# The opening of a two-layer kernel: a new order on four engines, four sums moved to VectorE, scratch of its own for two rows

## The chip, the cores and the metric

One core of a Trainium2 chip. The metric is the device time of one execution in microseconds; before the change it is 1047.22 us, the median of 3 runs (1045.82 to 1048.94).

## The reference

The input is 4096 rows of 512 numbers (2 x 2048 x 512, float32). With LN a layer norm without weights:

```python
# attention layer
h = LN(x)
Q, V = h @ Wq.T + bq, h @ Wv.T + bv          # 16 heads of 32
logits = einsum('bhtd,lhd->bhtl', Q, latent) / sqrt(32)   # 64 latent keys
w = softmax(top_k(logits, 4))                 # weights of the 4 largest
a = einsum('bhtk,bhtkd->bhtd', w, selected latent rows) + V
x = x + LN(a @ Wo.T + bo)
# FFN layer, 512 -> 2048 -> 512
ternary(W) = clip(round(W / s), -1, 1) * s,   s = mean(|W|) + 1e-8
hid = silu(LN(x) @ ternary(W_up).T) * (LN(x) @ ternary(W_gate).T)
x = x + LN(hid @ ternary(W_down).T)
```

K is not used by the result.

## The kernel before

The rows are worked in 8 chunks of 512, a chunk being 4 tiles (t = 0 to 3) of 128 rows. One pass of the body does the attention of chunk i beside the FFN of chunk i - 1: "first" (attention of chunk 0 alone, called the opening here), "second", five passes "mid", "last" and "tail". The change touches "first" alone. To keep accuracy with float16 matmuls, each operand is split into a high and a low half (hi, lo): ScalarE (ACT) writes hi, GpSimd (POOL) or VectorE (DVE) writes lo as the difference, and TensorE (PE) adds three products.

Each engine has its order written out by hand in `body`, and semaphores link them: an engine runs its list strictly in order, so an instruction that waits holds all behind it. The parts of the opening, by the kernel's names:

- The first layer norm, the maxima of the weights and powers of two from them (`powers`, L1328), the splits of Wq, Wv, Wo (`weights_hi` L818 on ACT, `weights_lo` L1417 on DVE; index 0, 1, 2), Q in two halves of 256 rows (`q_half`), logits into PSUM (`logits`, L560), copied to Lb by ACT.
- The chain of a tile t on four engines. DVE: `maxes(t, b)` (8 MAX8 each, L1462), `slots(t)` (L1469, differences of the top four), `replace(t, b)` (8 MATCH_REPLACE8 each, L1484, marks the top four in Lr; after b = 1 it signals `replaced`), `sums(t)` (L1490 to L1500, needs `exp4(t)` of ACT), `select(t)` (L1505, needs `exps(t)`). POOL: `shift(t)` (L1170, after `replaced`), `normalise(t)` (L1177, after `select`), `probs_lo(t)` (L1160). ACT: `exp4(t)` (L904), `exps(t)` (L908, after `shift`), `probs_hi(t)` (L921, after `normalise`). SyncE (SP) then transposes the weights by DMA: `pt(t)`, L421. `probs_hi(2)` first waits for the transposes of tiles 0 and 1, and before the change `probs_hi(3)` for those of tiles 0 to 2.
- `v(m)` on PE (V of all rows), `weigh_half(h)` (L611, needs two transposed tiles each), `vw_half(m, h)` on ACT (L867, L871), `low_a_half(m, h)` on POOL (L1155), then `wo(t)` on PE (L646), the output projection: wo(0), wo(1) need the four `low_a_half(m, 0)`, wo(2), wo(3) the four of h = 1.
- On DVE `y_a(t)` (L1557 to L1565, reads wo(t)) and `y_b(t)` (L1577 to L1585, residual and statistics), between them `rstd_y(t)` on POOL, after them `rstd_x(0, t)` on POOL and `y_c(0, t)` on DVE, and the rows of the second norm (`t2_rows`, `t2_lo`, transposes L366).
- The rows of the next chunk: `ln1_stat(1)`, `ln1_rstd_of(1)` on POOL, `ln1_biases(1)`, then per tile `s1_rows(1, t)` on ACT (L777, L790), `s1_lo(1, t)` on POOL (L1206), and a transpose by SP (`s1`, L366) into XT. The second pass begins on PE with Q of chunk 1, which needs all four transposed tiles.
- The scales of the ternary weights: sums of magnitudes of 24 pieces of 128 x 1024 (`abs_sum(n)`; pieces 0 to 7 W_up, 8 to 15 W_gate). ACT does one as an activation with an accumulated sum (L838), DVE as a reduction (L1350). `tern_total(w)` adds eight pieces on DVE, `total` on PE adds over the partitions (L525), `tern_scale_of(w)` makes the scale, `round_to(n)` on DVE and `sign(n)` on ACT write a ternary piece. Q of the second pass also waits for `tern_scale_of(1)` (`tern_step` 2), for its bank of PSUM.

`split_buffers` gives the buffers of a row and its halves. Before the change tiles 2 and 3 of chunk 1 use those of tiles 0 and 1 again, so ACT waits for the low half of tile t - 2:

```python
elif kind == "first":
    wait(act, x_lo, i + c, TT, t - 1)
```

## Time and profile before

| what | value |
|---|---|
| median of 3 runs | 1047.22 us |
| the profiled execution, its time | 1049.91 us |
| its span in the profile | 1048.1 us |
| mean granted TensorE clock | 0.977 of full |

The profile is of one execution. Times in its rows are microseconds from the start of the span. An engine's idle time before an instruction stands in square brackets with what ended it; "issue" means that the profile shows nothing that it waited for. A busy PE may be at half clock; the granted clock tells.

### The profile page before, as it was taken

What the parts mean: (1) busy time and instruction counts of PE and PEld (TensorE: products, weight loads), DVE (VectorE), ACT (ScalarE), POOL (GpSimd) and SP (SyncE); (2) the same over time, 40 slices, a digit from 0 to 9 for tenths busy, and PEclk for the clock granted to TensorE, in tenths of its full rate; (3) what the DMA queues carried; (4) which work ended last, traced back from release to release, by engine and by line L of the source; (5) the groups of instructions that cost most, each with busy time, mean ns of one, the idle gap of its engine ahead of it and who ended that gap; (6) DMA issues with size and microseconds to landing.
All of it is one profiled execution on the core that took longest, in us unless ns stands there. A gap on an engine that the chain in (4) does not pass through costs nothing.

```text
span 1048.1 us, 17870 instructions
## 1 busy us (share of the span) xinstructions
PE 969.4 (92%) x5738; PEld 472.0 (45%) x5738; DVE 736.0 (70%) x2668; ACT 515.4 (49%) x803; POOL 542.8 (52%) x448
## 2 busy tenths in 40 slices
PE   2474998899999999999999999999999999989997
PEld 1331544345444454445444454445444454435443
DVE  6997889746993769836994768836894768835331
ACT  4867887245454355345444455345453445323321
POOL 2466346664565446554565446654566445633332
PEclk9786999999999999999999999999999999999999
DMA  8944502434115321243023321253023311212001
GB/s 252 395 101 91 162 1 61 113 89 101 19 23 102 71 71 20 50 110 91 13 38 89 76 76 20 40 119 92 11 40 72 88 31 21 41 41 62 1 0 41
DMA packets 149335, 76.94 MB, mean 73 GB/s; under 512 B 135825, under 2 KB 135825, under 8 KB 148113
## 3 DMA queue, kind: packets, MB, share of 16 engines
q1 hardware_dynamic: 149264, 76.18, 29.1%
q8 instruction: 23, 0.38, 0.1%
q14 instruction: 48, 0.39, 0.1%
HBM read 34.21 MB, written 8.39 MB: 41 GB/s over the span
## 4 chain that ended last, share of the span: by engine, by line
PE 76%; DVE 10%; issue 4%; ACT 4%; DMA 3%; POOL 2%; SPq 0%; POOLq 0%; DVEq 0%; ACTq 0%
PE ug L668 36%; PE ug L685 17%; PE ring L534 12%; PE ring L646 6%; PE ring L582 2%; DVE Lr L1484 2%; DMA PT<-halves 1%; PE ug L534 1%; PE ring L626 1%; DVE v L1462 1%; DVE ugt L1447 1%; ACT TU L844 1%; DMA x_in<-in_x 1%; DVE halves L1442 1%; ACT TG L844 0%
## 5 line engine op out<-in xcount | busy, mean ns | idle before, releaser
L1183 POOL TENSOR_TENSOR hT<-ugt,hT 128x512 f16<-128x512 f32 x128 | 168.0, 1312 | 164.2 <-ACT hT L953 164.2
L668 PE MATMUL ug<-X1T,TU 128*128 128x512 f16 (+1 forms) x1152 | 245.1, 356 | 7.2 <-DVE ugt L1452 6.3
L668 PE MATMUL ug<-X1T,TG 128*128 128x512 f16 (+1 forms) x1152 | 244.8, 355 | 0.0
L685 PE MATMUL ug<-TD,hT 128*128 128x512 f16 x960 | 213.6, 383 | 3.2 <-issue 3.2
L946 ACT ACTIVATE ugt<-ug,cu 128x512 f32<-128x512 f32 x128 | 87.9, 687 | 204.0 <-PE ug L668 203.2
L668 PEld LDWEIGHTS ug<-X1T,TU 128*128 128x128 f16 x1152 | 110.5, 98 | 116.1 <-DVE ugt L1452 5.5
L668 PEld LDWEIGHTS ug<-X1T,TG 128*128 128x128 f16 x1152 | 112.7, 98 | 108.6
L1447 DVE SCALAR_TENSOR_TENSOR ugt<-ugt,ug 128x512 f32<-128x512 f32 x128 | 87.3, 682 | 100.3 <-ACT ugt L946 99.4
L685 PEld LDWEIGHTS ug<-TD,hT 128*128 128x128 f16 x960 | 94.0, 99 | 120.6 <-issue 11.0
L1484 DVE MATCH_REPLACE8 Lr<-v,Lb 128x68 f32<-128x68 f32 x512 | 102.4, 213 | 0.2 <-issue 0.2
L1517 DVE BATCH_NORM_STATS2 stf<-ug 128x6 f32<-128x512 f32 x30 | 20.8, 694 | 109.3 <-PE ug L685 109.3
L1452 DVE SCALAR_TENSOR_TENSOR ugt<-ugt,ug 128x512 f32<-128x512 f32 x128 | 87.9, 687 | 4.4
L534 PE MATMUL ring<-XT,wq_hi 128*128 128x512 f16 (+1 forms) x288 | 80.5, 367 | 8.4 <-DVE wq_lo L1420 5.8
L1177 POOL TENSOR_TENSOR p<-Lb,r 128x1024 f32<-128x1024 f32 x32 | 60.8, 1901 | 48.3 <-issue 33.0
L1170 POOL TENSOR_TENSOR Lb<-Lb,v 128x1024 f32<-128x1024 f32 x32 | 62.3, 1947 | 44.4 <-DVE Lr L1484 44.4
L953 ACT ACTIVATE hT<-ugt 128x512 f16<-128x512 f32 x128 | 79.6, 622 | 3.7 <-DVE ugt L1452 3.7
L1462 DVE MAX8 v<-Lb 128x8 f32<-128x64 f32 x512 | 68.9, 210 | 0.4
L534 PE MATMUL ring<-XT,wv_hi 128*128 128x512 f16 x224 | 66.6, 379 | 0.0
L921 ACT ACTIVATE halves<-p 128x1024 f16<-128x1024 f32 x31 | 32.5, 1048 | 50.9 <-POOL p L1177 40.1
L534 PE MATMUL ring<-XT,wq_lo 128*128 128x512 f16 (+1 forms) x144 | 52.9, 367 | 0.0
L646 PE MATMUL ring<-wo_hi,qaT_hi 128*128 128x512 f16 x128 | 50.2, 392 | 2.5 <-POOL qaT_lo L1155 1.9
L804 ACT ACTIVATE xn<-x,nbx,rsx 128x512 f32<-128x512 f32 x28 | 22.7, 809 | 56.3 <-DVE nbx L1591 37.5
(193 smaller groups left out, 1464.8 us busy)
## 6 DMA issues: line engine op xcount, KB each, us to landing
out_dram<-Lr SPq DMA_DIRECT2D x32, 256.0 KB, 3.1
x_in<-in_x SPq DMA_DIRECT2D x7, 1024.0 KB, 5.5
x<-in_x SPq DMA_DIRECT2D x28, 256.0 KB, 3.3
PT<-in_Wd SPq DMA_DIRECT2D x8, 512.0 KB, 8.1
hT<-in_Wu SPq DMA_DIRECT2D x4, 512.0 KB, 9.4
hT<-in_Wg SPq DMA_DIRECT2D x4, 512.0 KB, 15.1
x_in<-in_Wd SPq DMA_DIRECT2D x4, 512.0 KB, 5.2
x_in<-in_x SPq DMA_DIRECT2D x4, 256.0 KB, 4.2
```

The costliest lines, as they stand in the source:

```text
L534: last = pe.matmul(bank[:, cols], wT[w][a][:, k, m * P:(m + 1) * P], XT[:, b, k, cols], start=(n == 1), stop=(stop and n == 3 * KD), skip_ ...
L646: last = pe.matmul(ring[:, bank, :], qaT[a][:, k, t * P:(t + 1) * P], wT[2][b][:, k, :], start=(n == 1), stop=(n == 3 * KD))
L668: last = pe.matmul(ug[:, 2 * (e % 2) + s, cols], w[:, k, e * P:(e + 1) * P], X1T[:, b, k, cols], start=(k == 0 and b == 0), stop=(k == KD ...
L685: last = pe.matmul(down_bank(kind, t), hT[:, a, e, t * P:(t + 1) * P], td[:, e, :], start=(e == 0 and a == 0), stop=(e == NE - 1 and a == 1))
L946: act.activation(ugt[:, e % 2, :], ug[:, 2 * (e % 2), :], ACT.Tanh, scale=cu[:, 0:1]).then_inc(tanh_ready, 1)
L953: act.activation(hT[:, 0, e, :], ugt[:, 2 + e % 2, :], ACT.Copy).then_inc(h_hi, 1)
L1170: pool.tensor_tensor(buf, buf, v8[:, t % 2, :, 0:1].broadcast_to([P, H, NL]), ALU.subtract).then_inc(shifted, 1)
L1183: pool.tensor_tensor(hT[:, 1, e, :], ugt[:, 2 + e % 2, :], hT[:, 0, e, :], ALU.subtract).then_inc(h_lo, 1)
L1447: dve.scalar_tensor_tensor(out=ugt[:, e % 2, :], in0=ugt[:, e % 2, :], scalar=1.0, in1=ug[:, 2 * (e % 2), :], op0=ALU.add, op1=ALU.mult).t ...
L1452: dve.scalar_tensor_tensor(out=ugt[:, 2 + e % 2, :], in0=ugt[:, e % 2, :], scalar=HS, in1=ug[:, 2 * (e % 2) + 1, :], op0=ALU.mult, op1=ALU ...
L1462: last = dve.max(v8[:, t % 2, h, :], Lb[:, t % 2, h, 0:NL])
L1484: last = dve.match_replace(Lr[:, h, :], v8[:, t % 2, h, :], Lb[:, t % 2, h, :], HIT)
```

## The change

- **DVE:** `sums(t)` stands between `replace(t, 0)` and `replace(t, 1)`; `weights_lo(1)` moves ahead of `select(0)`, `latV_lo` to behind `replace(1, 1)`, `weights_lo(2)` to behind `replace(3, 1)`. The sums of pieces 12 to 15 come from ACT to DVE, behind `select(3)` and `ln1_biases(1)`; `y_a(0)` and `y_a(1)` stand ahead of `tern_total(0)`, `y_a(2)` and `y_a(3)` ahead of `tern_total(1)`.
- **ACT:** `exp4(0)` ahead of `logits(1)`, the remaining sums spread anew, the rows of tiles 2 and 3 ahead of `vw_half(m, 1)`, with no wait for buffers, and a wait for two transposes ahead of `sign(0)`.
- **POOL:** `shift(3)` behind `probs_lo(2)` and ahead of all `low_a_half(m, 0)`; `normalise(3)` between the first and the last two of these; `rstd_x(0, 0)` between `low_a_half(1, 1)` and `low_a_half(2, 1)`, `rstd_x(0, 1)` between `s1_lo(1, 2)` and `s1_lo(1, 3)`.
- **PE:** the second `total` of the guards ahead of `logits(0, 1)`; `weigh_half(1)` ahead of the total of W_up; the total of W_gate behind `wo(3)`.
- **Buffers:** tiles 2 and 3 of chunk 1, and the weights of attention of tile 3, lie in parts of TU, which is free until `sign(0)`.

```diff
--- before.py
+++ after.py
@@ -262,8 +262,8 @@
         junk = xn[:, :].bitcast(F16)
         late_junk = ring[:, 0:2, :].rearrange("p b t -> p (b t)")
 
-        ASUM_DVE = (0, 1)
-        ASUM_ACT = (16, 17, 18, 19) + tuple(range(2, 16)) + tuple(range(20, 24))
+        ASUM_DVE = (0, 1, 12, 13, 14, 15)
+        ASUM_ACT = (16, 17, 18, 19) + tuple(range(2, 12)) + tuple(range(20, 24))
         TERN_ORDER = (0, 8, 1, 9, 4, 12, 2, 10, 5, 13, 3, 11, 6, 14, 22, 23, 16, 17, 7, 15, 20, 21, 18, 19)
 
         def after_tern(*pieces):
@@ -298,6 +298,8 @@
             if kind == "first" and c == 0:
                 return (qaT[t // 2][:, :, :].rearrange("p k t -> p (k t)").bitcast(F32)[:, (t % 2) * D:(t % 2 + 1) * D],
                         PT[:, 0, 2 * t:2 * t + 2, :].rearrange("p k t -> p (k t)"))
+            if kind == "first" and t >= 2:
+                return TU[:, 2 * D * t:2 * D * t + 2 * D].bitcast(F32), TU[:, 2 * D * t + 4 * D:2 * D * t + 6 * D]
             if kind == "first":
                 return Lb[:, t % 2, 0:D // NL, 0:NL], out_buf[t % 2].bitcast(F16)
             return xn[:, :], halves[:, t % 2, :]
@@ -306,6 +308,8 @@
 
             if kind == "first" and t == 1:
                 return row[:, :, :].rearrange("p a d -> p (a d)").bitcast(F16).rearrange("p (s d) -> p s d", s=2)
+            if kind == "first" and t == 3:
+                return TU[:, 0:4 * D].rearrange("p (s d) -> p s d", s=2)
             return halves[:, :, :]
 
         def wide(v, rows):
@@ -692,9 +696,9 @@
                     for m in range(KD):
                         q_half(m, 0)
                     q_half(0, 1)
-                    logits(0, 1)
                     pe.wait_ge(qa32_ready, KD)
                     total(guard_sums(1), mg[:, 2:4], mg_ready, 2, ma_ready)
+                    logits(0, 1)
                     q_half(1, 1)
                     q_half(2, 1)
                     pe.wait_ge(sc_step, 7)
@@ -705,14 +709,14 @@
                     weigh_half(0)
                     wo(0)
                     wo(1)
+                    weigh_half(1)
                     wait(pe, l_ready, i, 8, 8)
                     total(weight_sum(0), tot[:, 0:1], tot_ready, 1, tota_ready)
-                    weigh_half(1)
-                    wait(pe, y_ready, i, TT, 1)
-                    total(weight_sum(1), tot[:, 1:2], tot_ready, 2, tota_ready)
                     wo(2)
                     pe.wait_ge(tern_step, 1)
                     wo(3)
+                    wait(pe, y_ready, i, TT, 1)
+                    total(weight_sum(1), tot[:, 1:2], tot_ready, 2, tota_ready)
                     return
                 if att:
                     for m in range(KD):
@@ -768,7 +772,7 @@
 
                         wait(act, p_ready, i, TT, 3 + t)
                     elif kind == "first":
-                        wait(act, x_lo, i + c, TT, t - 1)
+                        pass
                     elif t:
                         wait(act, x_lo, i + c, TT, t)
                     else:
@@ -783,6 +787,8 @@
                     elif kind == "first" and t < 2:
 
                         wait(act, p_raw, i, TT, TT)
+                    elif kind == "first":
+                        pass
                     elif t < 2:
                         wait(act, p_t, i + c, 16 * TT, 0)
                     else:
@@ -796,7 +802,7 @@
                     if t:
                         wait(act, x1_lo, i + c, TT, t)
                     elif kind == "first":
-                        act.wait_ge(asum_done, ASUM_ACT.index(2 * NPIECE - 1) + 1)
+                        act.wait_ge(asum_done, ASUM_ACT.index(11) + 1)
                     elif nxt:
                         wait(act, x_lo, i + 1, TT, TT)
                     else:
@@ -913,7 +919,7 @@
                     if kind == "first" and t == 1:
                         act.wait_ge(latV_split[1], 1)
                         wait(act, scales, 0, 1, 2)
-                    elif t:
+                    elif t and not (kind == "first" and t == 3):
                         wait(act, p_t, i, 16 * TT, 16 * t)
                     for s in range(2):
                         if t == 0 and ffn:
@@ -972,54 +978,51 @@
                     q_half(1, 1)
                     q_half(2, 1)
                     q_half(3, 1)
+                    exp4(0)
                     logits(1)
-                    exp4(0)
                     weights_hi(1)
                     exps(0)
                     latV_hi()
                     abs_sum(16)
+                    exp4(1)
                     abs_sum(17)
-                    exp4(1)
                     probs_hi(0)
                     logits(2)
                     abs_sum(18)
-                    weights_hi(2)
                     exps(1)
                     abs_sum(19)
-                    abs_sum(2)
-                    abs_sum(3)
                     exp4(2)
-                    abs_sum(4)
-                    abs_sum(5)
+                    weights_hi(2)
                     probs_hi(1)
                     logits(3)
-                    abs_sum(6)
-                    abs_sum(7)
+                    abs_sum(2)
                     exps(2)
-                    abs_sum(8)
+                    abs_sum(3)
+                    abs_sum(4)
                     exp4(3)
+                    abs_sum(5)
+                    probs_hi(2)
                     vw_half(0, 0)
                     vw_half(1, 0)
+                    exps(3)
                     vw_half(2, 0)
                     vw_half(3, 0)
-                    probs_hi(2)
-                    exps(3)
-                    abs_sum(9)
-                    abs_sum(10)
-                    abs_sum(11)
-                    abs_sum(12)
                     probs_hi(3)
                     s1_rows(1, 0)
                     s1_rows(1, 1)
-                    abs_sum(13)
-                    abs_sum(14)
-                    abs_sum(15)
+                    abs_sum(6)
+                    abs_sum(7)
+                    s1_rows(1, 2)
+                    s1_rows(1, 3)
                     vw_half(0, 1)
                     vw_half(1, 1)
                     vw_half(2, 1)
                     vw_half(3, 1)
-                    s1_rows(1, 2)
-                    s1_rows(1, 3)
+                    abs_sum(8)
+                    abs_sum(9)
+                    abs_sum(10)
+                    abs_sum(11)
+                    act.wait_ge(x_t[0], 32)
                     sign(0)
                     t2_rows(0, 0)
                     sign(8)
@@ -1223,25 +1226,29 @@
                     shift(1)
                     probs_lo(0)
                     normalise(1)
+                    shift(2)
                     probs_lo(1)
-                    shift(2)
                     normalise(2)
-                    for m in range(KD):
-                        low_a_half(m, 0)
+                    probs_lo(2)
                     shift(3)
-                    probs_lo(2)
+                    low_a_half(0, 0)
+                    low_a_half(1, 0)
                     ln1_rstd_of(1)
                     normalise(3)
+                    low_a_half(2, 0)
+                    low_a_half(3, 0)
+                    probs_lo(3)
                     rstd_y(0)
-                    probs_lo(3)
-                    rstd_y(1)
                     s1_lo(1, 0)
                     s1_lo(1, 1)
+                    rstd_y(1)
+                    low_a_half(0, 1)
+                    low_a_half(1, 1)
                     rstd_x(0, 0)
+                    low_a_half(2, 1)
+                    low_a_half(3, 1)
+                    s1_lo(1, 2)
                     rstd_x(0, 1)
-                    for m in range(KD):
-                        low_a_half(m, 1)
-                    s1_lo(1, 2)
                     s1_lo(1, 3)
                     rstd_y(2)
                     rstd_y(3)
@@ -1352,8 +1359,8 @@
             def tern_total(w):
                 pieces = range(NPIECE * w, NPIECE * w + NPIECE)
                 dve.wait_ge(asum_done, max(ASUM_ACT.index(n) + 1 for n in pieces if n in ASUM_ACT))
-                if w == 0:
-                    dve.wait_ge(own_asum, len(ASUM_DVE))
+                if w < 2:
+                    dve.wait_ge(own_asum, (2, len(ASUM_DVE))[w])
                 dve.reduce_sum(tot[:, w:w + 1], asum[:, NPIECE * w:NPIECE * w + NPIECE], AX.X).then_inc(tot_ready, 1)
 
             def tern_scale_of(w):
@@ -1616,50 +1623,52 @@
                     maxes(0, 1)
                     slots(0)
                     replace(0, 0)
+                    sums(0)
                     replace(0, 1)
                     maxes(1, 0)
                     maxes(1, 1)
-                    sums(0)
+                    weights_lo(1)
                     select(0)
                     slots(1)
                     replace(1, 0)
+                    sums(1)
                     replace(1, 1)
-                    weights_lo(1)
+                    latV_lo()
                     maxes(2, 0)
                     maxes(2, 1)
-                    sums(1)
                     select(1)
                     slots(2)
                     replace(2, 0)
+                    sums(2)
                     replace(2, 1)
-                    latV_lo()
-                    weights_lo(2)
                     maxes(3, 0)
                     maxes(3, 1)
-                    sums(2)
                     select(2)
                     slots(3)
                     replace(3, 0)
+                    sums(3)
                     replace(3, 1)
+                    weights_lo(2)
                     ln1_stat(1)
+                    select(3)
+                    ln1_biases(1)
+                    for n in range(12, 16):
+                        abs_sum(n)
+                    y_a(0)
+                    y_a(1)
                     tern_total(0)
-                    sums(3)
-                    select(3)
-                    y_a(0)
-                    ln1_biases(1)
-                    y_a(1)
                     tern_scale_of(0)
                     round_to(0)
                     y_b(0)
                     y_b(1)
-                    tern_total(1)
                     y_c(0, 0)
                     y_c(0, 1)
+                    y_a(2)
+                    y_a(3)
+                    tern_total(1)
                     tern_scale_of(1)
                     round_to(8)
-                    y_a(2)
                     t2_lo(0, 0)
-                    y_a(3)
                     y_b(2)
                     t2_lo(0, 1)
                     y_c(0, 2)
```

## Rows read from the trace of the kernel before

**Rows 1.** The head of the page and its busy times.

```profile
span 1048.1 us, 17870 instructions
...
PE 969.4 (92%) x5738; PEld 472.0 (45%) x5738; DVE 736.0 (70%) x2668; ACT 515.4 (49%) x803; POOL 542.8 (52%) x448
```

**Rows 2.** Stretches: PE, PEld, DVE, ACT, POOL busy (x), PEclk, DMA share, GB/s.

```profile
78.00:104.00 26.00, 11.33 (x85) 5.22 (x84) 18.59 (x43) 20.98 (x35) 16.61 (x17) 0.71 0.49 92
...
104.00:130.00 26.00, 26.00 (x190) 15.24 (x188) 21.20 (x42) 22.12 (x31) 9.90 (x8) 0.96 0.53 163
```

**Rows 3.** Chain that ended last, opening: start us, us, what.

```profile
71.06 7.45 PE ring L646 x24
...
89.94 0.91 PE ug L611 x18
...
96.10 1.17 POOL Lr L1206
...
98.83 3.11 DMA XT<-Lr
...
102.19 12.22 PE ring L534 x48
```

**Rows 4.** Timeline of DVE, opening: start us, us, instruction, idle before it.

```profile
27.86 1.21 DVE L1350 TENSOR_REDUCE asum<-ugt 128x1 f32<-128x1024 f32 x1
...
31.61 2.12 DVE L1462 MAX8 v<-Lb 128x8 f32<-128x64 f32 x16
...
34.06 0.09 DVE L1484 MATCH_VALUE_LOAD Lr<-v,Lb 128x8 f32 x1
...
37.24 2.12 DVE L1462 MAX8 v<-Lb 128x8 f32<-128x64 f32 x16
...
53.34 0.20 DVE L1490 TENSOR_REDUCE s<-d 128x16 f32<-128x64 f32 x1
...
53.96 1.16 DVE L1505 SCALAR_TENSOR_TENSOR Lb<-Lr,Lb 128x1024 f32<-128x1024 f32 x1
```

**Rows 5.** Line L1420, the low halves of the weights: duration ns min/median/max.

```profile
L1420 DVE SCALAR_TENSOR_TENSOR wv_lo<-TG,upw,wv_hi x4: 740/1580/2609, 45.1 to 50.7; 128x512 f16<-128x512 f32 x4
...
L1420 DVE SCALAR_TENSOR_TENSOR wo_lo<-TG,upw,wo_hi x4: 747/747/747, 59.1 to 61.1; 128x512 f16<-128x512 f32 x4
```

**Rows 6.** Timeline of POOL beside those instructions.

```profile
45.28 2.37 POOL L1170 TENSOR_TENSOR Lb<-Lb,v 128x1024 f32<-128x1024 f32 x1 [1.55 <-DVE Lr L1484]
...
47.61 2.57 POOL L1160 TENSOR_TENSOR halves<-p,halves 128x1024 f16<-128x1024 f32 x1
...
60.44 3.42 POOL L1160 TENSOR_TENSOR row<-p,row 128x1024 f16<-128x1024 f32 x1 [3.28 <-ACT row L921]
```

**Rows 7.** Timeline of ACT: the copies of logits(1).

```profile
35.28 1.25 ACT L898 ACTIVATE Lb<-ug,clo 128x512 f32<-128x512 f32 x2
```

**Rows 8.** Line L421, transposes of the weights of attention.

```profile
DMA to landing us min/median/max: 4.3/4.4/9.4
```

**Rows 9.** Timeline of POOL, end of the opening.

```profile
70.25 1.48 POOL L1155 TENSOR_TENSOR qaT_lo<-x_kept,qaT_hi 128x256 f16<-128x256 f32 x2
...
73.44 1.93 POOL L1170 TENSOR_TENSOR Lb<-Lb,v 128x1024 f32<-128x1024 f32 x1
...
83.14 2.12 POOL L1160 TENSOR_TENSOR halves<-p,halves 128x1024 f16<-128x1024 f32 x1 [1.74 <-ACT halves L921]
...
88.56 0.98 POOL L1124 TENSOR_TENSOR rsx<-vax,nh 128x1 f32<-128x1 f32 x1
```

**Rows 10.** Timeline of DVE, rows of the output projection and of the second norm.

```profile
78.78 0.74 DVE L1557 SCALAR_TENSOR_TENSOR row<-ring,clo,bo_b 128x512 f32<-128x512 f32 x1
...
80.84 0.74 DVE L1557 SCALAR_TENSOR_TENSOR row<-ring,clo,bo_b 128x512 f32<-128x512 f32 x1
...
85.74 0.74 DVE L1577 SCALAR_TENSOR_TENSOR x<-row,rsy,x 128x512 f32<-128x512 f32 x1
...
87.66 1.49 DVE L1577 SCALAR_TENSOR_TENSOR x<-row,rsy,x 128x512 f32<-128x512 f32 x1
```

## The prediction

> **What bounds the kernel.** I read the page first: PE is busy for 92% of the span [rows 1]. That says little of the opening, so I cut the start into stretches: from 78 to 104 us PE works 11.33 of 26 us, at a granted clock of 0.71 (part of it at 1.2 GHz, not 2.4), while from 104 to 130 us it is busy all through, at 0.96 [rows 2]. The border is the start of Q of chunk 1 at 102.19. What the change can win is therefore how much earlier that start comes; everything behind it moves with it, as long as PE has its inputs. The chain says what ends last before it: the transposed weights of tiles 2 and 3 let PE do `weigh_half(1)` at 89.94, and behind it come ACT, POOL's `s1_lo` at 96.10, and the transpose issued at 98.83 that lands 3.11 later [rows 3]. The weights of tile 3 hang on `probs_lo(3)`, which POOL starts at 83.14, and that on `shift(3)` at 73.44 [rows 9], at the end of four tiles' work in line on DVE.
>
> Third, the timelines of DVE and POOL, for waits that are no idle time. The four low halves of Wv take up to 2609 ns each, those of Wo 747 [rows 5]. Beside Wv's lie two POOL instructions of 2.37 and 2.57 us [rows 6], where the same kinds take 1.93 and 2.12 alone [rows 9]. Operations of DVE with two operands in SBUF and operations of POOL take turns: one stands while the other runs. Maxima, replacements and reductions show no such stretch.
>
> **Part by part.** I walk the chain anew, each time a start or an end in the changed kernel.
>
> *Start.* PE makes the guard's total before the logits, so `powers(1)` is done before the first copy of logits lands; `maxes(0)` starts at about 31.0, not 31.61. Maxima and slots take 2.45, sixteen replacements 3.18, so half of them 1.6; sums 0.6; select 1.2 [rows 4]. Half of tile 0 is replaced at 35.0. `sums(0)` now stands there and waits for `exp4(0)`, which ACT can start where `logits(1)` stood, at 35.28 [rows 7]: done at 35.5. With sums 36.2, second half 37.8, against 37.24 before [rows 4]. The move costs 0.5 here.
>
> *`weights_lo(1)`.* `maxes(1)` ends at 39.9. The splits follow while POOL waits for `select(0)`, so they take 2.7, as Wo's did [rows 5], not the 6.3 from 45.1 to the end of the last: done at 42.6. V can start 9 us earlier. I price that at nothing: V is used by `weigh_half(0)`, which waits for `pt(1)`. The price is paid by `select(0)`: 43.8, then tile 1 is replaced at 43.8 + 0.3 + 1.6 + 0.6 + 1.6 = 47.9, against 45.28 for the shift that it releases [rows 6].
>
> *Tiles 1 to 3.* `shift(1)` from 48.0, held 0.25 by `latV_lo`, ends at 50.2; `exps(1)`, some 1.1, at 51.3. POOL is then in `probs_lo(0)` until 52.3, and `select(1)` has two SBUF operands: it ends at 53.2, before at 55.1 [rows 4]. Tile 2 is replaced at 53.2 + 4.1 = 57.3, `shift(2)` ends at 59.4, `probs_lo(1)` at 61.5; `select(2)` is held by it and ends at 62.5; tile 3 is replaced at 66.6. `logits(3)` stands behind the splits of Wo on ACT, but `select(2)` comes later than its maxima either way, so I cost that at nothing.
>
> *The meeting at 67.* `pt(1)` is issued at 61.65 and lands after 4.4 [rows 8], at 66.1; `probs_hi(2)` ends at 67.1. POOL now has `probs_lo(2)` ahead of `shift(3)`, and DVE is in `weights_lo(2)` from 66.6 to 69.3. Two outcomes are in the trace. (B) DVE keeps the port through its four: `probs_lo` beside Wo's splits took 3.42 instead of 2.12, so it stood 1.3 us, longer than one split of 0.75 [rows 5, 6, 9]. Then `probs_lo(2)` ends at 71.3 and `shift(3)` at 73.3, 2.1 earlier than before. (A) They alternate, as at 45 us: `shift(3)` ends at 71.9, but the splits at 73.5, and `ln1_stat(1)` and `select(3)` behind them end at 77.7. I take B: it is the same pair of instructions. The Trainium skill (SBUF — State Buffer, Who interferes with whom) says that whoever issues first holds the pair for the whole instruction and the other blocks; taken strictly, the turn would pass after each split, which is A, and Q would come at 102.3 to 103.3. The trace bears it out at 45 us and not at 60.
>
> *Out of the chain, by B.* `exps(3)` 74.4; two `low_a_half` 1.5 [rows 9], 74.8; `select(3)` 76.0; POOL's `ln1_rstd_of(1)`, 1.0 as its like [rows 9], 77.0; `normalise(3)`, as long as a shift, 78.9; the other two `low_a_half` 80.4; `probs_lo(3)` 82.5, before 85.3 [rows 9]. `probs_hi(3)` no longer waits for a transpose: the wait was in the old 83.14. `pt(3)` lands at 87.0, `weigh_half(1)` ends at 87.9, before 90.85 [rows 3]: 2.9 won.
>
> *Four sums on DVE.* 4 x 1.2 [rows 4] from 77.1 to 81.9. Behind them wait `y_a(0)`, `y_a(1)` and the total of W_up. PE ends `wo(0)` at about 82 (`low_a_half(3, 0)` at 80.4 is its last input) and `wo(1)` at 86: 24 matmuls took 7.45, the first of them at half clock [rows 3], and these start from idle too. So the sums cost nothing; `y_a(1)`, 2.0 [rows 10], ends at 88.0, and the total at 88.2 meets the end of `weigh_half(1)`. On ACT four sums less are hidden: it waits for `weigh_half(1)`.
>
> *Where the gain goes.* Rows 2 and 3 of chunk 1 no longer wait on ACT, but `s1_lo(1, 2)` stands on POOL behind `low_a_half(3, 1)`, and that behind `rstd_x(0, 0)`, which needs `y_b(0)`, `round_to(0)` and the total of W_up. 88.4 total, 88.9 scale, 90.0 rounded (with 0.4 of port), `y_b(0)` 1.9 [rows 10] and 0.4, 92.3; `rstd_x` 1.0, 93.3; two `low_a_half` 94.8; `s1_lo` 1.17 [rows 3], 96.0; `rstd_x` 0.8, 96.8; `s1_lo` 98.0. The last transpose is issued at 98.2 instead of 98.83: Q could start at 101.5. The other condition of Q is new in place: `tern_scale_of(1)` comes after `wo(3)` and `y_a(3)`. `wo(2)` ends at 96.0; `wo(3)` at 97.9 at full clock or 99.9 at half; then 2.0 for `y_a(3)` and 0.8 for total and scale: 100.8 to 102.7. I take Q at 102.0, 0.2 earlier. By A each step from `select(3)` on is 0.7 to 1.4 later: Q at 102.3 to 103.3.
>
> **Sum.** The profiled execution took 1049.91 us around its span of 1048.1 [rows 1]; 0.2 less is 1049.7. The median of the three runs is 2.7 lower, so against it the forecast is 1047.22 - 0.2 = 1047.0. A measurement of this kernel can tell about 0.3% from no change, 3.1 us.
>
> **Rivals.** (1) *Faster: the collisions don't happen.* If `select(1)`, `select(2)` and `probs_lo(2)` each get the port at once, `pt(3)` lands up to 4 us earlier than I have it, `wo` and the rest behind it too, and Q starts at 98. That is 4.2 less; and PE would idle less before Q, so up to 1 us of its half clock goes [rows 2]. 1043.0 to 1042. For it: DVE's own work in line shrinks by the 3.6 us of Wv. Against it: new placements put DVE's two-operand work beside POOL's three times.
>
> (2) *Slower: the total of W_gate becomes the bound.* Place: PE's list, `total` behind `wo(3)`, DVE's `y_a(3)` ahead of `tern_total(1)`. It decides from the point where `wo(3)` ends later than 99.4, and each us beyond is a us of time. If A comes, `y_b(0)` is held by the port as well and `wo(2)`, `wo(3)` run at half clock (the 24 in 7.45 had half clock for some 4 us; the other 3.4 would double [rows 3]), `wo(3)` ends at 102.5 and Q starts at 105.4: 3.2 more, 1050.4. For it: `wo(2)` now gets its inputs in two pairs with `rstd_x` between, so PE idles inside it. Against: B, and a clock that was up in half of this stretch [rows 2].
>
> (3) *A instead of B:* 0.1 to 1.1 more, 1047.3 to 1048.3, within what counts as the same. This is also the sentence on the skill's rule.
>
> (4) The change does what it says, but the second pass, with roundings and tiles on DVE, gives or takes another 1 us by the same port; that is in the range.
>
> **Numbers.** B 0.40, A 0.22, rival 1 0.22, rival 2 0.16. Same is B and A, 0.62; faster 0.22; slower 0.16. The range takes the forecast with 1.5 us of unknown on each side of A and B, and reaches to rival 1's upper half and to rival 2's price with 0.6 above it: 1042.5 to 1051.0.
>
> **What would show it.** Splits of Wv of 0.75 each from 40 us and V at 43. `select(1)` longer than 1.2. POOL's `probs_lo(2)` at 67 of over 4 us (B), or `weights_lo(2)` spread over 7 us (A). `probs_lo(3)` ending at 82.5, `weigh_half(1)` at 87. `rstd_x(0, 0)` with POOL idle before it, released by DVE. Q at 101.5 to 102.7, released by the scale or the transpose about alike. I am wrong if Q starts before 99 or after 105, or if it starts where I say and the time differs by over 3 us all the same: then the second pass made it.

## The result and the profile after

The changed kernel took 1050.76 us (median of 8 runs, 1049.45 to 1052.49), the kernel before beside it 1047.93 (8 runs, 1045.82 to 1049.64): a ratio of 1.0028, 95% interval 1.0019 to 1.0038. Run again as `after_again` (11 runs, beside other runs of before) it took 1050.84 and the ratio was 1.0018 (1.0009 to 1.0027). One run of before in that batch, of 2652.3 us, was slow and is left out of the ratios. The change makes the kernel slower by 2 to 3 us. I had forecast 1047.0, no difference. Line numbers from L1120 on are now 3 to 7 higher.

The head of the page after, with its busy times:

```profile
span 1048.6 us, 17859 instructions
...
PE 969.0 (92%) x5738; PEld 470.9 (45%) x5738; DVE 739.3 (71%) x2672; ACT 510.7 (49%) x795; POOL 542.5 (52%) x448
```

It answers to [rows 1] and tells nothing: no engine's work has changed by more than 5 us. The profiled execution took 1050.42 us, only 0.5 more than that of before, against 2.8 in the medians. So I did not compare whole spans. Two things blur them. The kernel's first work starts at another time in each execution (the first norm's `rs` in POOL between 8.40 and 9.89 us over all my profiles), and far behind the change some executions have a short stretch at a lower granted clock. Stretch 920 to 925 us, in before, after and after_again (PE, PEld, DVE, ACT, POOL busy, PEclk, DMA share, GB/s):

```profile
920.00:925.00 5.00, 4.02 (x54) 1.50 (x55) 0.00 (x0) 2.97 (x5) 1.61 (x2) 0.69 0.19 63
```
```profile
920.00:925.00 5.00, 1.99 (x51) 0.90 (x51) 0.00 (x0) 0.91 (x2) 0.00 (x0) 1.00 0.69 155
```
```profile
920.00:925.00 5.00, 2.32 (x48) 0.94 (x48) 0.00 (x0) 0.75 (x2) 0.00 (x0) 0.76 0.59 136
```

In all three PE has just waited some 3 us for transposed weights; PE's row behind that wait, before and then after:

```profile
920.98 0.63 PE L626 MATMUL ring<-PT,latV_hi 64*32 64x512 f16 x16 [3.00 <-DMA PT<-halves]
```
```profile
923.15 0.63 PE L630 MATMUL ring<-PT,latV_hi 64*32 64x512 f16 x16 [3.02 <-DMA PT<-halves]
```

Behind this wait the granted clock fell in before and after_again and not in after, and the change touches nothing there. Before's profile lost about 1.6 us by it: counted as below, its lead over after is 2.66 us at the output store near 802 us and 1.04 at the last. From here on I count each mark of a profile from the start of that first `rs` (before 9.89, after 9.39, after_again 9.69):

```
us from the start of the first rs      before   after   after_again
weigh_half(1) on PE                     80.05   78.59    78.72
first matmul of Q of chunk 1            92.30   94.52    94.75
first sign of the second pass (ACT)    105.80  108.15   108.40
first store of the output              197.75  200.05   200.30
```

The opening gains 1.5 us up to `weigh_half(1)` and then loses 3.7 before Q. From Q on the 2.2 us stay, 2.3 at the first store, and that is the size of the ratio. Where they arise stands in the chain that ended last, 66 to 104 us, after (start us, us, what):

```profile
66.53 6.60 DVE wo_lo L1427 x4
73.12 2.39 DVE st L1404 x4
...
76.24 1.14 DVE Lb L1512
...
77.41 0.83 POOL rs L1127
78.24 1.86 POOL p L1180
80.11 0.64 POOL qaT_lo L1158
...
80.79 6.12 PE ring L650 x18
...
93.49 1.00 POOL rsx L1127
94.49 0.64 POOL qaT_lo L1158
...
95.17 5.76 PE ring L650 x18
...
102.90 0.17 DVE tot L1364
```

In [rows 3] the chain went over `weigh_half(1)`, `s1_lo` and a transpose to Q. Now it enters DVE at the four splits of Wo, 6.60 us where they took 2.73 before, goes on through what stands behind them, then over PE's `wo(2)` and `wo(3)`, and ends at the total of W_gate. Three rows of PE's timeline show the price at the end of it (start us, us, instruction, idle before it and who ended that):

```profile
95.17 0.61 PE L650 MATMUL ring<-wo_hi,qaT_hi 128*128 128x512 f16 x1 [2.11 <-POOL qaT_lo L1158]
103.21 0.35 PE L529 MATMUL ring<-tot,ones 128*128 128x1 f32 x2 [2.29 <-DVE tot L1364]
103.91 0.59 PE L538 MATMUL ring<-XT,wq_hi 128*128 128x512 f16 x2 [0.34 <-DVE sw L1369]
```

PE stands 2.11 us inside `wo(2)`, then 2.29 for `y_a(3)` and the sum behind it, and 0.34 for the scale: Q follows the scale, not the transposes (the last is issued near 98.6 and lands some 3.0 later, at about 101.6). The stretches of [rows 2], after:

```profile
78.00:104.00 26.00, 15.70 (x95) 6.10 (x96) 19.57 (x42) 18.89 (x32) 16.45 (x19) 0.73 0.40 62
104.00:130.00 26.00, 24.92 (x188) 14.75 (x188) 22.12 (x36) 22.64 (x32) 9.75 (x8) 1.00 0.63 172
```

PE does 4.4 us more in the first stretch than before, and yet Q starts later: `wo(0)` and `wo(1)`, which ran at 71 to 78 us before, now wait for `normalise(3)` and what follows it on POOL (4.70 us, until 80.79) and lie in it too.

The splits and POOL beside them. Line L1427, duration ns min/median/max, then POOL's timeline, then DVE's, all after:

```profile
L1427 DVE SCALAR_TENSOR_TENSOR wv_lo<-TG,upw,wv_hi x4: 731/742/743, 39.5 to 41.5; 128x512 f16<-128x512 f32 x4
...
L1427 DVE SCALAR_TENSOR_TENSOR wo_lo<-TG,upw,wo_hi x4: 746/1783/2609, 66.4 to 72.0; 128x512 f16<-128x512 f32 x4
```
```profile
66.99 2.17 POOL L1163 TENSOR_TENSOR halves<-p,halves 128x1024 f16<-128x1024 f32 x1 [2.56 <-ACT halves L927]
69.12 2.38 POOL L1173 TENSOR_TENSOR Lb<-Lb,v 128x1024 f32<-128x1024 f32 x1
71.46 2.19 POOL L1158 TENSOR_TENSOR qaT_lo<-x_kept,qaT_hi 128x256 f16<-128x256 f32 x2
```
```profile
66.44 0.75 DVE L1427 SCALAR_TENSOR_TENSOR wo_lo<-TG,upw,wo_hi 128x512 f16<-128x512 f32 x1
...
71.97 1.15 DVE L1427 SCALAR_TENSOR_TENSOR wo_lo<-TG,upw,wo_hi 128x512 f16<-128x512 f32 x1
...
76.15 1.22 DVE L1512 SCALAR_TENSOR_TENSOR Lb<-Lr,Lb 128x1024 f32<-128x1024 f32 x1
78.28 1.85 DVE L1416 SCALAR_TENSOR_TENSOR nb<-mv,rs 128x4 f32<-128x4 f32 x1 [0.91 <-POOL rs L1127]
80.05 4.58 DVE L1357 TENSOR_REDUCE asum<-hT 128x1 f32<-128x1024 f32 x4
```

Read the four splits against POOL: the first runs alone (0.75); the second stands through `probs_lo(2)`, the third through `shift(3)`, the fourth for part of a `low_a_half` (1.15). The four of Wv, moved to 39.5 us, take 2.72 instead of 6.28: that part of the change does what it should. The row at 78.28 is a surprise: four elements a partition, 1.85 us, all through POOL's `normalise(3)` (78.21 to 80.11).

### The profile page after: what moved, and what is told of

Same layout as the page of the kernel before. It is cut to its first block, busy times and chain, and to the rows that moved or that the text cites. A ratio compares the mean times of both kernels' runs of the same rounds, so it can differ in the third digit from the quotient of the medians.

```text
span 1048.6 us, 17859 instructions
## 1 busy us (share of the span) xinstructions
PE 969.0 (92%) x5738; PEld 470.9 (45%) x5738; DVE 739.3 (71%) x2672; ACT 510.7 (49%) x795; POOL 542.5 (52%) x448
## 4 chain that ended last, share of the span: by engine, by line
PE 64%; DVE 17%; issue 6%; ACT 5%; POOL 5%; DMA 3%; POOLq 0%; SPq 0%; DVEq 0%; ACTq 0%
PE ug L672 33%; PE ug L689 13%; PE ring L538 9%; PE ring L650 6%; DVE Lr L1491 3%; PE ring L586 2%; DVE ugt L1454 1%; DMA PT<-halves 1%; DVE Lb L1512 1%; DVE v L1469 1%; POOL halves L1209 1%; DVE stx L1587 1%; DVE halves L1449 1%; DVE x L1584 1%; DVE row L1564 1%
## 5 line engine op out<-in xcount | busy, mean ns | idle before, releaser
L689 PE MATMUL ug<-TD,hT 128*128 128x512 f16 x960 | 211.3, 380 | 3.2 <-issue 3.2
L1491 DVE MATCH_REPLACE8 Lr<-v,Lb 128x68 f32<-128x68 f32 x512 | 102.3, 211 | 0.0
L1173 POOL TENSOR_TENSOR Lb<-Lb,v 128x1024 f32<-128x1024 f32 x32 | 62.5, 1953 | 48.1 <-DVE Lr L1491 48.1
L538 PE MATMUL ring<-XT,wv_hi 128*128 128x512 f16 x224 | 66.6, 379 | 0.0
L650 PE MATMUL ring<-wo_lo,qaT_hi 128*128 128x512 f16 x128 | 50.8, 397 | 0.0
```

What stands on the lines that cost most here:

```text
L538: last = pe.matmul(bank[:, cols], wT[w][a][:, k, m * P:(m + 1) * P], XT[:, b, k, cols], start=(n == 1), stop=(stop and n == 3 * KD), skip_ ...
L650: last = pe.matmul(ring[:, bank, :], qaT[a][:, k, t * P:(t + 1) * P], wT[2][b][:, k, :], start=(n == 1), stop=(n == 3 * KD))
L689: last = pe.matmul(down_bank(kind, t), hT[:, a, e, t * P:(t + 1) * P], td[:, e, :], start=(e == 0 and a == 0), stop=(e == NE - 1 and a == 1))
L1173: pool.tensor_tensor(buf, buf, v8[:, t % 2, :, 0:1].broadcast_to([P, H, NL]), ALU.subtract).then_inc(shifted, 1)
L1491: last = dve.match_replace(Lr[:, h, :], v8[:, t % 2, h, :], Lb[:, t % 2, h, :], HIT)
```

## The experiments

**after_again** is the changed kernel itself, beside e1 to e3; its numbers stand above.

> The changed kernel as it is, on this chip, as the yardstick of the other three. Q of chunk 1 starts at 103.9 us in its first profile, 1.7 later than before, and what follows keeps that: 1.5 to 3 us slower than before in the median.

All ratios are against before, run beside each kernel. "From rs" means the marks of the table above. The theory: (a) the turn-taking at 67 us makes `select(3)` late, and (b) `wo(3)`, `y_a(3)` and the total of W_gate, now behind one another, carry that to Q. The rivals: the four sums on DVE, the second pass, POOL's order.

**e1_splits_in_gap**, against (a): Wo's splits go between `sums(3)` and the last eight replacements, when POOL has little to do.

```diff
 sums(3)
+weights_lo(2)
 replace(3, 1)
-weights_lo(2)
```

> weights_lo(2) ahead of replace(3, 1), where POOL waits for the transpose. Theory 1 (the meeting of weights_lo(2) with probs_lo(2) and shift(3) cost DVE 4 us in the chain): the four splits take 2.7 us instead of 6.7, select(3) ends about 3.5 us earlier, weigh_half(1) comes at about 84 instead of 88, and Q at about 100. Rival (the total of W_gate behind wo(3) sets the start of Q by itself, through ACT's last magnitude sums, which end at 97.4): Q gains under 1 us. Time by theory 1: 3 to 4 us less than the changed kernel.

Ratio 0.9986 (0.9977 to 0.9995), median 1047.14. The splits take 2.65 us, `weigh_half(1)` is at 75.07 from rs and Q at 91.34, 3.2 earlier than in the changed kernel. So the alternation costs 3.2 us of Q, and 0.3 to 0.4% of the time (0.9986 against 1.0018 and 1.0028). One list entry turns the change from a loss to a small gain. The marks of the one profile show the loss gone but no gain over before: Q is 1.0 us earlier, the first sign (105.93) and the first store (197.87) stand where before's do. Part (b) is still there, PE waits 2.28 for the total:

```profile
99.85 0.56 PE L529 MATMUL ring<-tot,ones 128*128 128x1 f32 x2 [2.28 <-DVE tot L1364]
100.75 1.01 PE L538 MATMUL ring<-XT,wq_hi 128*128 128x512 f16 x2 [0.34 <-DVE sw L1369]
```

**e2_total_early**, against (b): on PE the total goes ahead of `wo(3)`, on DVE the sum, scale and rounding ahead of `y_a(3)`.

```diff
 wo(2)
-pe.wait_ge(tern_step, 1)
-wo(3)
 wait(pe, y_ready, i, TT, 1)
 total(weight_sum(1), ...)
+pe.wait_ge(tern_step, 1)
+wo(3)
...
+tern_total(1)
 y_a(2)
-y_a(3)
-tern_total(1)
 tern_scale_of(1)
 round_to(8)
+y_a(3)
```

> The total of W_gate ahead of wo(3) on PE, tern_total(1) ahead of y_a(2) on DVE, the scale and round_to(8) between y_a(2) and y_a(3). Theory 2 (Q waits for the scale alone, the transposed rows have landed before): Q starts at 101.9 to 102.2, when the last transpose of chunk 1's rows lands, 1.8 us earlier, and the time is 1.8 us less than the changed kernel, about that of before. Rival (the time of the second norm's rows or of the second pass decides, not Q): no change.

Q is at 92.35 from rs and the first sign at 106.07, both 2.1 to 2.2 earlier than in the changed kernel. The timed ratio does not show it: 1.0017 (1.0006 to 1.0028), median 1049.72 with runs from 1047.73 to 1052.87. So the profile says that (b) holds Q by 2.2 us; that it is worth 2.2 us of time is not shown by this run. In the profile the gain stays: the store near 802 us is 2.44 earlier from rs than in after, the last store 1.67 earlier than in after_again, which like e2 has the lower clock at 920. Before Q, PE now waits 0.97 for DVE's reading of `wo(3)` in `y_a(3)`.

**e3_both**, e1 and e2 together.

> Both edits. If both theories hold, the transposed rows come at about 98 and the scale is not later: Q at 98 to 99.5, 4 to 5.5 us less than the changed kernel and 2 to 3.5 less than before. If the magnitude sums of ACT, which now wait less, still end at about 95 and hold the total, Q comes at 99 or later.

Ratio 0.9982 (0.9973 to 0.9991), median 1046.59; Q at 90.34 from rs, first sign at 105.20, first store at 197.12. The gains do not add. The total of W_gate now waits 0.91 for ACT's own sums. In the second pass PE's first FFN matmuls wait 1.13 for the transposed rows of the second norm (0.91 in the changed kernel), and the later ones, at 120.71, 1.16 for a product that DVE makes from their results (0.17 there): a second queue is right behind the first.

**d1_no_dve_sums**, the rival of the sums. The kernel leaves the four sums of `abs_sum(12)` to `(15)` out, and the scale of W_gate is made from ACT's four alone.

```diff
-for n in range(12, 16):
-    abs_sum(n)
```

> The changed kernel without the four magnitude sums on DVE; the scale of W_gate is then made from the other four sums alone. Theory (they lie beside PE's wo(0) and wo(1) and cost nothing): y_a(1) starts when wo(1) ends, as now, Q at about 103.9, no change of time. Rival (they are in the chain): up to 4.6 us less before y_a(0), Q up to 2 us earlier.

Ratio 1.0019 (1.0010 to 1.0027); Q at 94.51 from rs, against 94.52 with the sums. `y_a(0)` and `y_a(1)` only wait for PE instead (3.44 and 1.57 us in place of 0 and 0.40). The 4.58 us of sums cost nothing, as forecast, and this rival falls.

**d2_before_wv_ahead**, one part of the change alone: before, with Wv's splits ahead of `select(0)`.

```diff
 sums(0)
+weights_lo(1)
 select(0)
...
 replace(1, 1)
-weights_lo(1)
```

> The kernel before with one part of the change alone: weights_lo(1) ahead of select(0). Theory (port): the four splits of Wv take 2.7 us instead of 6.3, so maxes(2) starts at about 47.5 instead of 51.3; select(1) may meet probs_lo(0) and lose 1; tile 3 is done 2.5 to 3.5 us earlier, weigh_half(1) at about 87, Q at 99 to 100, 1.5 to 3 us less than before. Rival (the transposes and ACT hold tile 3 anyway): no change.

Ratio 0.9986 (0.9977 to 0.9995), median 1047.35; Q at 91.53 from rs, 0.8 earlier than before. This one move alone is as good as e1, the whole change with its fault mended. It fell short of its expectation all the same: Wv's splits take 2.65 in place of 6.28, but `weigh_half(1)` is only 0.8 earlier from rs (79.26), where Q was to come 2 to 3 us earlier. Where the rest went isn't shown. It also gives a second case like [rows 6], in POOL's and DVE's rows:

```profile
58.63 2.96 POOL L1160 TENSOR_TENSOR row<-p,row 128x1024 f16<-128x1024 f32 x1 [3.74 <-ACT row L921]
```
```profile
L1420 DVE SCALAR_TENSOR_TENSOR wo_lo<-TG,upw,wo_hi x4: 743/743/745, 56.9 to 58.9; 128x512 f16<-128x512 f32 x4
```

POOL asks in the third split (58.20 on) and stands some 0.8 us, through the fourth: none of the four is held. So [rows 5, 6] were no accident of one profile, and yet the same pair came out the other way at 67 us.

**d3_low_a_ahead**, POOL's order: the changed kernel, with the inputs of `wo(2)` ahead of the second norm's root.

```diff
-rstd_x(0, 0)
 low_a_half(2, 1)
 low_a_half(3, 1)
+rstd_x(0, 0)
```

> The changed kernel with low_a_half(2, 1) and (3, 1) ahead of rstd_x(0, 0) on POOL. Theory (wo(2) and with it the total of W_gate hang on POOL's place behind the statistics of y_b(0)): wo(2) runs without its gap of 2.1 us, wo(3) ends 2 to 2.5 us earlier at about 98.5, Q at 101.5 to 102, 1.5 to 2.4 us less than the changed kernel. Rival: ACT's last magnitude sums (97.4) and the rows' transposes hold Q, under 1 us.

Ratio 0.9997 (0.9987 to 1.0007), median 1047.93; Q at 93.13 from rs, 1.4 earlier. The hole of 2.11 us inside `wo(2)` is gone (0.26), and 1.3 us of it come back as a longer wait for the total:

```profile
100.99 0.56 PE L529 MATMUL ring<-tot,ones 128*128 128x1 f32 x2 [3.59 <-DVE tot L1364]
101.89 1.01 PE L538 MATMUL ring<-XT,wq_hi 128*128 128x512 f16 x2 [0.34 <-DVE sw L1369]
```

So three steps share the loss, and each of e1, e2 and d3 takes one away: 3.2, 2.2 and 1.4 us of Q, more in sum than the 2.2 lost against before, as they lie in one line and overlap.

**f1_reordered**, what follows for the kernel. From e3: both totals on PE between `weigh_half(1)` and `wo(2)`; ACT's sums spread over its earlier waits, its `t2_rows(0, 0)` ahead of the first sign; on POOL `s1_lo(1, 2)` and both `low_a_half` ahead of `rstd_x(0, 0)`, and the roots of tiles 2 and 3 in the order of their tiles; on DVE, as a diff against e3:

```diff
 tern_total(0)
+tern_total(1)
+y_b(0)
 tern_scale_of(0)
+tern_scale_of(1)
 round_to(0)
-y_b(0)
+round_to(8)
 y_b(1)
...
```

> A version of its own, from e3_both: ACT does four more magnitude sums where it waits for POOL, so that both totals are made together behind y_a(1); low_a_half(2, 1), (3, 1) and the rows of chunk 1 ahead of rstd_x(0, 0) on POOL; t2_rows(0, 0) ahead of sign(0); t2_lo(0, 0) and y_b(2) ahead of y_a(3) on DVE. Theory: what follows e3 is held by the order, not by work: wo(3) ends at 95, Q at 95 to 97, 2 to 4 us less than e3_both, 3.5 to 5.5 less than before. Rival: the second norm's rows and DVE's roundings in the second pass take most of it back, under 1 us less than e3_both.

Ratio 0.9960 (0.9947 to 0.9973), median 1043.96; Q at 87.93 from rs, 4.4 earlier than before, the first store 3.7 earlier. Faster than both kernels.

**f2_last_tile_first**, f1 with `s1_lo(1, 3)` ahead of `rstd_x(0, 0)` as well.

> The reordered kernel (f1), with s1_lo(1, 3) also ahead of rstd_x(0, 0) on GpSimd, because its Q began at 97.32 us after a wait of 2.04 us for the transposes of those rows. Theory (the rows of the last tile set Q there): s1_lo(1, 3) ends 1.0 us earlier, Q starts near 96.3, and the first sign of the second pass is up to 1 us earlier: 0.995 to 0.996 against before. Rival (second norm's rows set what follows Q): Q starts earlier, but the first sign of the second pass does not, as rstd_x(0, 0) is 1.15 us later, and the time is that of f1 or up to 1 us longer.

Ratio 0.9951 (0.9937 to 0.9965), median 1043.22. Q at 86.78 from rs, first sign at 101.48, 1.15 and 0.65 earlier than in f1: the theory. The two ratios overlap, so that f2 beats f1 is shown by the marks alone. PE's row of Q, and the stretches, f2:

```profile
96.05 0.59 PE L538 MATMUL ring<-XT,wq_hi 128*128 128x512 f16 x2 [1.54 <-DMA XT<-TU]
```
```profile
78.00:104.00 26.00, 21.35 (x129) 8.91 (x128) 22.41 (x54) 17.36 (x30) 14.95 (x17) 0.88 0.50 82
```

PE is busy 21.35 us of the stretch where the changed kernel had 15.70, at a granted clock of 0.88 in place of 0.73. The transposes end last before Q again, as in [rows 3].

**x3_shift_ahead**, the last rival: is it POOL's order, `shift(3)` behind `probs_lo(2)`, rather than DVE's?

```diff
-probs_lo(2)
 shift(3)
+probs_lo(2)
```

> The changed kernel, with shift(3) ahead of probs_lo(2) on GpSimd. Theory (the lost time is that of VectorE's four splits and of ln1_stat behind them): the splits still take about 6.6 us beside GpSimd's two large operations, ln1_stat still ends near 76 and select(3) stays at 76, so the ratio stays that of the changed kernel, 1.001 to 1.004 against before. Rival (the lost time is that of GpSimd's order, shift(3) behind probs_lo(2)): select(3) starts 2 us or more earlier, near 73.5, and the ratio falls to 1.000 or less.

The splits take 6.68 us again, `select(3)` starts at 76.32; ratio 1.0012 (1.0002 to 1.0021), within the changed kernel's. So what makes `select(3)` late is DVE's own queue, splits and `ln1_stat(1)`. (This profile has its first sign 2.5 us later than the changed kernel's, from rs, where Q is 1.5 later; the timed runs show no such loss.)

**x1_request_in_first_split** and **x2_request_in_third_split** ask what decides who gets the turn, by one profile each. x1 is an edit of before, x2 of the changed kernel, whose last eight replacements are cut into heads 8 to 10 and 11 to 15:

```diff
 latV_lo()
-weights_lo(2)
 maxes(3, 0)
+weights_lo(2)
```
```diff
 sums(3)
-replace(3, 1)
+replace(3, 1, 8, 11)
 weights_lo(2)
+replace(3, 1, 11, 16)
```

> The kernel before, with maxes(3, 0) moved in front of weights_lo(2), so that GpSimd's probs_lo(1), which asked for its turn at 60.44 us between the second and the third of the four splits of Wo and then waited through them, now asks in the first split (splits at about 60.2 to 62.8 if they are not held). Theory P (the place of the request in the run of splits decides): as in the changed kernel at 66.99 us, probs_lo(1) starts at once and ends near 62.6, and the four splits take 6 to 7 us in place of 2.73. Rival B (this kernel's DVE keeps its turn whatever the place, the changed kernel differs by something else): the splits take 2.7 us and probs_lo(1) lasts more than 4 us.

> The changed kernel, with the second replacing of tile 3 cut in two (heads 8 to 10, the four splits of Wo, heads 11 to 15), so that the splits start about 1 us earlier and GpSimd's probs_lo(2) asks at about 67.0 us in the third of them. Theory P (place decides): the splits take 2.7 us, probs_lo(2) waits about 1 us for the fourth to end, shift(3) starts near 70 and select(3) near 75.6. Rival (the changed kernel's other moves decide): probs_lo(2) starts at once, the splits that are left alternate with GpSimd, wo_lo takes 5 us or more and select(3) starts after 78.

x1 missed its aim: the maxima waited 1.89 us for ACT, so `probs_lo(1)` started beside an idle DVE at 60.31, and it was `shift(2)` that asked in the first split. It was let in behind it, and one split stood 2.42: 4.65 us in all, and Q 1.4 us later than before (93.66 from rs). Its one time is 1050.91, beside a median of 1048.59 for before. x2 hit it, and theory P falls:

```profile
66.71 2.52 POOL L1163 TENSOR_TENSOR halves<-p,halves 128x1024 f16<-128x1024 f32 x1 [2.55 <-ACT halves L927]
```
```profile
L1427 DVE SCALAR_TENSOR_TENSOR wo_lo<-TG,upw,wo_hi x4: 742/744/2608, 65.2 to 67.2; 128x512 f16<-128x512 f32 x4
```

POOL asked in the third split (66.51 on), stood 0.4 us, and the fourth stood 1.9 for it. In d2 it asked in the third as well and waited through the fourth. So the place in the run doesn't decide. Nor does the time left in it: POOL asked 0.11 us before DVE's next split in after and 0.46 in x2, and was let in, 0.23 in d2, and was not. What x2 does show is the price per turn: with `shift(3)` kept out of the splits (its tile was not marked yet) they take 4.59 instead of 6.68, and Q comes at 92.67 from rs, 1.9 earlier than in the changed kernel: 2.1 us off the splits, 1.9 off Q. Its one time is 1047.44.

## Why the prediction was wrong

**Right, up to 67 us.** The walk met the trace within about 0.4 us: Wv's splits 2.72 (2.7), `shift(1)` 47.57 to 49.7 (48.0 to 50.2), `select(1)` to 52.9 (53.2), `shift(2)` from 57.30 (57.3), `probs_lo(1)` to 61.3 (61.5), `select(2)` to 62.4 (62.5), the splits of Wo from 66.44 (66.6). Both `select` were held, 2.06 and 2.04 us, so rival 1 had no basis. `sums(0)` waited for ACT and cost what I gave it. V ended earlier, but `weigh_half(0)` stood 10.49 us of idle time behind it, so this gave nothing.

**The step that failed: "The meeting at 67", "I take B: it is the same pair of instructions."** The trace of before had this pair come out one way at 45 us and the other at 60, and I let the nearer likeness decide, 0.40 to 0.22. What the runs showed was A, in all five profiles that keep this order (the two of the changed kernel, e2, d1, d3: 6.68 or 6.69 us for the four splits), and in x3 with the order turned. The Trainium skill's rule (SBUF — State Buffer, Who interferes with whom: whoever issues first holds the shared pair for the whole instruction, and the other blocks) described this meeting; [rows 6] at 60.44 and d2 at 58.63 it does not describe, as DVE's next split went ahead of a POOL instruction that was already waiting.

**My price of A was 1 to 2 us too small.** I had priced it as rival 3, "Q at 102.3 to 103.3". Q started at 103.91, and counted from rs 2.2 us later than before. I had missed one meeting, which did not reach Q, and mis-sized one term, which did:

- *`ln1_biases(1)`.* I had it cost nothing. It stands right behind `ln1_rstd_of(1)`, so it meets `normalise(3)` each time, and it stood 1.85 us. Behind it the sums ended at 84.6 and not at 81.9. d1 shows that this did not reach Q.
- *The pair from "Where the gain goes".* I had found both halves, `low_a_half(2, 1)` behind `rstd_x(0, 0)`, and the total of W_gate behind `wo(3)` and `y_a(3)`, and gave the first 93.3 (measured 93.49 for the start, 94.49 for the end) and the second "100.8 to 102.7" (measured 103.91). The mechanism is rival 2's, with its place and its waits: `wo(3)` ended at about 100.9, past my 99.4. Its price there, 105.4, was too high, since PE ran its last 18 matmuls in 5.76 us. The term that was mis-sized is `wo(3)`: I had 1.9 us for its twelve matmuls at full clock and 3.9 at half, where PE's rows have them 0.216 apart at one (2.6) and 0.427 at the other (5.1), as before's rows of L646 already do. That my late end for all 18 (from the first `low_a_half`, 94.1, to 99.9) comes to 5.8 all the same is luck, as the clock rose on the way.

PE's rows of `wo(2)` and `wo(3)`, after:

```profile
95.58 0.63 PE L650 MATMUL ring<-wo_lo,qaT_hi 128*128 128x512 f16 x1
...
98.14 0.63 PE L650 MATMUL ring<-wo_lo,qaT_hi 128*128 128x512 f16 x1
98.56 0.42 PE L650 MATMUL ring<-wo_hi,qaT_lo 128*128 128x512 f16 x1
...
100.55 0.38 PE L650 MATMUL ring<-wo_hi,qaT_lo 128*128 128x512 f16 x1
```

With the late end, 102.7, and A's own 1.2 us (`rstd_x(0, 0)` ended at 94.49 for 93.3), the sum gives the measured 103.9; I had added A to the single value that I took from the range, 102.0. I gave this pair 0.16 as a case apart; it was what A leads to, and rivals 2 and 3 should have been one case with one price between them.

**"Same" was wrong, the range held.** The range 1042.5 to 1051.0 contained 1050.76, near its end. The four sums on DVE cost nothing, right (d1). The step "PE ends `wo(1)` at 86" came out at 86.9, `weigh_half(1)` at 87.98 for 87.0, which is A's lateness. The granted clock of the stretch was 0.73 for 0.71, but from 60 to 100 us it was 0.60, against 0.74 before. V's matmuls, which before were at work until 64 us, now end at 55.4, and PE then idles 10.49 us ahead of `weigh_half(0)` and 6.03 ahead of `wo(0)` (columns as in [rows 2], before and after):

```profile
60.00:100.00 40.00, 21.58 (x166) 9.64 (x163) 31.75 (x105) 31.65 (x56) 30.01 (x25) 0.74 0.32 60
```
```profile
60.00:100.00 40.00, 18.52 (x143) 7.15 (x144) 34.03 (x86) 25.65 (x47) 26.92 (x23) 0.60 0.37 60
```

What the lower clock cost Q can be estimated from rows. At `wo(1)` it is at most 0.40 us, the wait of `y_a(1)` for it. At `wo(2)` and `wo(3)`, behind the wait of 2.11 us, it is about 1.7: eight matmuls 0.42 apart in place of 0.216.

**Still open.** Which of two waiting instructions gets the turn. POOL was let in at the next split's end at 45.28 (before), 62.41 (x1), 66.71 (x2) and 66.99 (after), and passed over at 60.44 (before) and 58.63 (d2). The last two have in common that the instruction is `probs_lo(1)` and that `latV_lo` ran directly ahead of the splits; no run here parts these. e2's missing gain is open too, and so is why x3's profile is later than its times.

## What to carry to other kernels

Where a trace shows the same pair of instructions meeting in two ways, price the worse one and place the work so that they don't meet: e1 moved four splits by eight instructions, into a time when GpSimd had nothing to do, and that was worth 3.2 us of the chain. When work is put late in a queue, look at every instruction behind it (here `ln1_stat`, `select(3)`, the sums) and at whom each releases. And when several waits lie in a line, mend all of them and then look again for the next: e3 gave 0.18%, f1, with the orders of all four engines redone around it, 0.4%.

## What the runs showed of the hardware that I had not expected

- A vector instruction of four elements a partition stood 1.85 us, through a whole GpSimd instruction (78.28, after). It has two operands in SBUF, as the splits and `select` have; being short did not spare it. The trace of before had such a case already, with a single tensor operand, so my rule of two operands was too narrow: `sums(2)` scales 16 elements a partition in 1.73 us beside `shift(2)` on POOL (63.82 to 65.75), where the same instruction takes 0.17 elsewhere (39.51). DVE's row stands below the list.
- A GpSimd instruction that waits is sometimes passed over by the next VectorE instruction, and sometimes not, at the same place of a run: 0.4 us of waiting in x2 and 0.8 in d2, both asked for in the third of four splits.
- A stretch at a lower granted clock comes in some executions of the same kernel and not in others, behind the same wait of PE of 3.0 us, 800 us behind anything that was changed (after_again 0.76 and after 1.00 from 920 to 925 us). Seven of my fourteen profiles have it there. It cost about 1.6 us in before. One profile's total is therefore no measure of a change of 2 us; marks counted from a common event show it better, though the timed runs of e2 and x3 did not follow theirs.

```profile
64.05 1.73 DVE L1498 TENSOR_SCALAR s4p<-s 128x16 f32<-128x16 f32 x1
```
